# Lora feed-forward with its first sum two tiles ahead, and an earlier key projection in attention

## The chip, the core and the metric

The kernel runs on one core of one Trainium2 chip. Its engines are TensorE (PE), VectorE (DVE), ScalarE (ACT) and GpSimd (POOL); SyncE (SP) only issues transfers here. Each works through its own instructions in order, and they wait for one another on semaphores. The metric is the device time of one execution in microseconds (us).

## What is computed

Two decoder layers over 2048 tokens of width 256, each an attention and a feed-forward, every one with a layer norm ahead and a residual sum behind. The change touches the feed-forward of the first layer (experts that are low-rank additions to one shared weight, two experts a token) and the start of the second layer's attention (16 heads of 128).

```python
# first layer, feed-forward
probs = jax.nn.softmax(x @ Wr + br, axis=-1)
w, idx = jax.lax.top_k(probs, K)                     # K = 2 experts of 8
base_h1 = x @ W1 + b1                                # 256 -> 1024
t1 = jnp.einsum('td,erd->ter', x, A1)                # rank 16
l1 = jnp.einsum('ter,efr->tef', t1, B1) * SCALING
a = gelu_new(base_h1[:, None, :] + l1)
ca = a * combine[:, :, None]
mix = ca.sum(axis=1)
t2 = jnp.einsum('tef,erf->ter', ca, A2)
l2 = jnp.einsum('ter,edr->td', t2, B2) * SCALING
out = mix @ W2 + combine.sum(-1, keepdims=True) * b2 + l2
...
# second layer, attention
q = _mxfp4_matmul(x, wq_codes, wq_scales) + bq       # codes * scales of 32 rows
k = _mxfp4_matmul(x, wk_codes, wk_scales) + bk
v = _mxfp4_matmul(x, wv_codes, wv_scales) + bv
scores = jnp.einsum('bqhd,bkhd->bhqk', q, k) / jnp.sqrt(jnp.float32(HEAD_DIM))
attn = jax.nn.softmax(scores, axis=-1)
out = jnp.einsum('bhqk,bkhd->bqhd', attn, v).reshape(B, S, NUM_HEADS * HEAD_DIM)
return _mxfp4_matmul(out, wo_codes, wo_scales) + bo
```

## The kernel before

The program is a row of stages: the first layer's attention, the Lora feed-forward (`lora_ffn`, its main part runs from about 294 to 521 us), the second attention (`attention`, from 521 us nearly to the end), the last feed-forward. A stage begins when all engines have ended the one before. Products whose precision matters are three matmuls of halves (`three`, L930 to L932: high by high, high by low, low by high).

**The main part of `lora_ffn`** works on four blocks `b` of 512 tokens, and in each on eight tiles `f` of 128 hidden features. Every tile needs two gelus, one for each of the token's two experts. Both are taken from one bank of PSUM, and the second is reached by adding to the first. TensorE does it with `first(f)` (nine matmuls: shared weight plus the first expert's low-rank part), and, when ScalarE has taken the first gelu, `second(f)` (three matmuls that add the second expert minus the first). Then ScalarE takes the second gelu. VectorE multiplies both by the gates (L1400) and adds them into `mix` (L1405), always both gelus of tile f and then `mix` of f. TensorE's `down_rank(f)` (L1322, two matmuls) needs both weighed gelus of tile f; it stands two tiles behind. When all eight tiles are through, TensorE multiplies `mix` by the second weight (L1346) and closes each of four row groups with a product of `t2` (L1350), and begins the next block.

The order is written out by hand. On TensorE it is

```python
first(0)
for f in range(NF):
    if f + 1 < NF:
        first(f + 1)
    second(f)
    if f >= 2:
        down_rank(f - 2)
```

On ScalarE it is both gelus of tile 0, both of tile 1 and so on, with three guests in blocks 1 to 3: after tile 1 a square root (`norm.deviation`, L93), which needs another table of functions, so that a table is loaded ahead of it and the gelu's again behind it; after tile 3 four normalised rows (L109); after tile 5 two copies (L124).

**Beside it, in the same 227 us, weights of the next attention are prepared** in 32 pieces, four (q, k, v, o) for each pair of heads. SP loads a piece (L1243, four L1246) into one of two buffers, GpSimd scales and splits it (`make_whole` L1270, `split_piece` L1278 and L1280; every other piece also two instructions of a bias, L1286, L1289), SP stores it (L1251) and loads the next but one. Of each o piece VectorE adds a product to `v_bias` (`weigh_bias`, L1390), and SP may not overwrite the buffer before: it waits for `v_bias_steps` with all later loads behind the wait. On VectorE `weigh_bias` stands ahead of tile 1 and ahead of tile 5 of each block (from block 0's tile 5 on), and its first instruction waits until GpSimd has scaled that piece.

**The start of `attention`.** TensorE projects the queries and keys of the first block of tokens (`project(0, 0, 0)`, `project(1, 0, 0)`), ScalarE and VectorE take the high and the low halves (`at_q_hi`, `at_q_lo`; the keys' halves bear the name `sw_gate_up_hi` and `_lo`, since they share that memory), and then step 0 begins: scores of queries 0 by keys of block 0, then the keys of block 1 (`project(1, 0, 1)`), then one product of `v_bias` (L1749). Step 1 begins with a wait for VectorE's sum `at_bo` and eight transposes (L117). A projection writes to one of two banks in turn, and waits until VectorE has read what was there two jobs ago (`claim`).

## Time and profile before

| | us |
|---|---|
| median of three runs | 2754.81 |
| lowest and highest | 2754.06, 2755.05 |
| the profiled execution | 2757.06 |
| its span, first to last instruction | 2755.3 |
| TensorE busy in the span | 2629.4 |
| four blocks of `lora_ffn`'s main part | 53.8, 57.6, 57.3, 58.0 |
| from there to the first score of step 1 of attention | 19.0 |

The span lies 1.8 us under the time of its execution, and that execution 2.25 us above the median. The views used are: busy time by stage, the waits summed by who waited for whom, and the order in time of each engine. In the last, a row is one or several equal instructions (`x4`; a matmul of whole float32 numbers counts twice), its start, its length from the first start to the last end, and in brackets the idle time ahead of it and what ended that. Ends of matmuls are modelled and overlap the next start; the distance of two starts is what one costs.

### The profile page before, as it was taken

Reading aid. Unit: us, or ns where it says so; the run is one execution under the profiler, and the core shown is the slowest. Engines: PE = TensorE matmul, PEld = TensorE weight load, DVE = VectorE, ACT = ScalarE, POOL = GpSimd, SP = SyncE. Lnnn points to the kernel's source line nnn. Section 1 sums busy time; section 2 is a strip of 40 time slices with the busy share of each in tenths; the row PEclk is TensorE's granted clock in tenths of the full one; section 3 lists DMA queues with packets and bytes.
Section 4 is the critical chain, followed back from the end, with each engine's and each line's share of the span. In section 5 each row is a group of like instructions: output and inputs, shape, how many; then the busy total and the mean of one; then the engine's idle time right before and its main releaser. Section 6 shows DMA issues by size and latency. Waiting matters only on the chain. (4 is left out here: it accounts for less than half of the span.)

```text
span 2755.3 us, 32467 instructions
## 1 busy us (share of the span) xinstructions
PE 2629.4 (95%) x11020; PEld 1871.1 (68%) x11021; DVE 2042.3 (74%) x2932; ACT 1618.5 (59%) x1891; POOL 2098.4 (76%) x1075
## 2 busy tenths in 40 slices
PE   7886999899999999999999999999999999997998
PEld 3333676677777777777777777777777777764765
DVE  6766655578888888888888888888888888885211
ACT  2323223367767776776677677767767766774122
POOL 2533555559988998998899899889988998996433
PEclk9998899999999999999999999999999999999999
DMA  2001445300000000000000000000000000004621
GB/s 68 0 0 54 122 131 145 114 16 5 8 5 19 6 8 16 5 9 5 16 5 12 16 5 9 5 16 5 12 12 9 8 5 9 1 20 83 228 61 47
DMA packets 76126, 90.52 MB, mean 33 GB/s; under 512 B 9310, under 2 KB 64865, under 8 KB 75970
## 3 DMA queue, kind: packets, MB, share of 16 engines
q1 hardware_dynamic: 72994, 81.30, 10.3%
q0 software_dynamic: 2976, 7.22, 0.9%
q8 instruction: 87, 1.43, 0.2%
q14 instruction: 69, 0.57, 0.1%
HBM read 62.39 MB, written 27.02 MB: 32 GB/s over the span
## 5 line engine op out<-in xcount | busy, mean ns | idle before, releaser
L1876 DVE TENSOR_TENSOR at_top<-at_psum_s,at_top 128x512 f32<-128x512 f32 x960 | 662.7, 690 | 214.9 <-ACT at_prob L1783 193.6
L1783 ACT ACTIVATE at_prob<-at_psum_s 128x1024 f32<-128x1024 f32 x512 | 521.5, 1019 | 451.8 <-PE at_psum_s L932 448.7
L2004 POOL TENSOR_TENSOR at_p_lo<-at_prob,at_p_hi 128x1024 fp32r<-128x1024 f32 x256 | 615.8, 2405 | 0.6 <-ACT at_p_hi L1797 0.6
L1865 DVE TENSOR_TENSOR at_prob<-at_prob,at_psum_m 128x1024 f32<-128x1024 f32 x512 | 603.6, 1210 | 0.0
L1789 ACT ACTIVATE at_prob<-at_prob 128x1024 f32<-128x1024 f32 x512 | 537.7, 1050 | 16.1 <-DVE at_prob L1865 13.0
L2033 POOL TENSOR_TENSOR at_acc<-at_acc,at_prob 128x1024 f32<-128x1024 f32 x189 | 452.9, 2396 | 82.3 <-ACT at_prob L1789 72.5
L1701 PE MATMUL at_psum_o<-at_prob,at_v 128*128 128x512 f32 x1024 | 482.0, 593 | 1.8 <-DVE at_oT_lo L1897 1.4
L2037 POOL TENSOR_TENSOR at_acc<-at_acc,at_prob 128x1024 f32<-128x1024 f32 x189 | 454.1, 2403 | 0.0
L930 PE MATMUL at_psum_s<-at_q_hi,sw_gate_up_hi 128*128 128x512 f32 x1024 | 403.4, 394 | 3.4 <-DVE sw_gate_up_lo L1857 3.4
L932 PE MATMUL at_psum_s<-at_q_hi,sw_gate_up_lo 128*128 128x512 f32 x1024 | 401.7, 392 | 0.0
L931 PE MATMUL at_psum_s<-at_q_lo,sw_gate_up_hi 128*128 128x512 f32 x1024 | 401.3, 392 | 0.0
L930 PE MATMUL at_psum_o<-at_p_hi,at_v_hi 128*128 128x512 f32 x512 | 298.3, 583 | 7.2 <-POOL at_p_lo L2004 6.9
L1701 PEld LDWEIGHTS at_psum_o<-at_prob,at_v 128*128 128x128 f32 x1024 | 184.9, 189 | 138.3 <-issue 118.4
L1797 ACT ACTIVATE at_p_hi<-at_prob 128x1024 fp32r<-128x1024 f32 x256 | 271.1, 1059 | 8.3 <-PE at_psum_o L932 0.2
L2028 POOL TENSOR_TENSOR at_acc<-at_prob 128x1024 f32<-128x1024 f32 x63 | 151.6, 2406 | 123.5 <-ACT at_prob L1789 119.3
L932 PEld LDWEIGHTS at_psum_s<-at_q_hi,sw_gate_up_lo 128*128 128x128 f32 x1024 | 192.9, 188 | 44.0
L930 PEld LDWEIGHTS at_psum_s<-at_q_hi,sw_gate_up_hi 128*128 128x128 f32 x1024 | 193.1, 189 | 40.8 <-DVE sw_gate_up_lo L1857 4.3
L931 PEld LDWEIGHTS at_psum_s<-at_q_lo,sw_gate_up_hi 128*128 128x128 f32 x1024 | 193.0, 188 | 36.4
L932 PE MATMUL at_psum_o<-at_p_hi,at_v_lo 128*128 128x512 f32 x512 | 202.0, 395 | 0.0
L931 PE MATMUL at_psum_o<-at_p_lo,at_v_hi 128*128 128x512 f32 x512 | 200.2, 391 | 0.0
L930 PEld LDWEIGHTS at_psum_o<-at_p_hi,at_v_hi 128*128 128x128 f32 x512 | 96.5, 189 | 89.0 <-issue 50.5
L1909 DVE SCALAR_TENSOR_TENSOR x_tok<-at_psum_w,at_rsum,x_tok 128x256 f32<-128x256 f32 x256 | 111.6, 478 | 52.8 <-PE at_psum_w L932 52.8
(349 smaller groups left out, 4415.8 us busy)
## 6 DMA issues: line engine op xcount, KB each, us to landing
ef_gate_up<-in_ef_gate_up SPq DMA_DIRECT2D x8, 1024.0 KB, 15.2
at_wq_split<-lf_pieces SPq DMA_DIRECT2D x8, 512.0 KB, 3.1
at_wk_split<-lf_pieces SPq DMA_DIRECT2D x8, 512.0 KB, 3.5
at_wv_split<-lf_pieces SPq DMA_DIRECT2D x8, 512.0 KB, 2.9
at_wo_split<-lf_pieces SPq DMA_DIRECT2D x8, 512.0 KB, 4.7
ef_down<-in_ef_down SPq DMA_DIRECT2D x8, 512.0 KB, 13.9
ef_rows_in<-ef_zeros SPq DMA_DIRECT2D x23, 128.5 KB, 8.6
ef_rows<-ef_rows_in SPq DMA_DIRECT2D x23, 128.5 KB, 2.2
```

The source lines that it names most:

```text
L930: nc.tensor.matmul(out, a_hi, b_hi, start=start, stop=False, **kw)
L931: nc.tensor.matmul(out, a_hi, b_lo, start=False, stop=False, **kw)
L932: return nc.tensor.matmul(out, a_lo, b_hi, start=False, stop=stop, **kw)
L1701: nc.tensor.matmul(psum_o[:], v[:, plain_at[kt], half], prob[u % 2][:, kt, :], start=(c == 0 and t == PAIRED[c]), stop=False)
L1783: nc.scalar.activation(pair(u, c, half), psum_s[:, 2 * half:2 * half + 2, :], ACT.Copy).then_inc(kept, 1)
L1789: nc.scalar.activation(part, part, ACT.Exp, scale=SCALE).then_inc(exp_done, 1)
L1797: nc.scalar.activation(p_hi[:, at:at + PAIRED[c], :], prob[u % 2][:, c * KPC:c * KPC + PAIRED[c], :], ACT.Copy).then_inc(p_hi_ready, 1)
L1865: nc.vector.tensor_tensor(part, part, psum_m[:].unsqueeze(1).to_broadcast([P, 2, BT]), ALU.subtract).then_inc(shifted, 1)
L1876: nc.vector.tensor_tensor(top[:, u % 2, :], psum_s[:, t, :], top[:, u % 2, :], ALU.max).then_inc(maxed, 1)
L2004: nc.gpsimd.tensor_tensor(p_lo[:, at, :], part, p_hi[:, at, :].bitcast(F32), ALU.subtract).then_inc(p_lo_ready, 1)
L2033: nc.gpsimd.tensor_tensor(acc2[:], acc2[:], pair(u, c, 0), ALU.add).then_inc(summed, 1)
L2037: nc.gpsimd.tensor_tensor(acc2[:], acc2[:], pair(u, c, 1), ALU.add).then_inc(summed, 1)
```

## The change

In `lora_ffn`, TensorE does `first(0)`, `first(1)`, and then for each f `first(f + 2)`, `second(f)`, `down_rank(f - 2)`. ScalarE takes its gelus in the order in which TensorE gives them: first of 0, first of 1, second of 0, first of 2, second of 1, and so on. The counts for which each engine waits follow from three small functions. The guests on ScalarE stand behind the same f of the loop as before. VectorE's and GpSimd's order stays. In `attention`, `project(1, 0, 1)` is moved from behind the scores of step 0 to ahead of them; ScalarE and VectorE take its result in the same place as before.

```diff
+            def first_at(f):
+                return f if f < 2 else 2 * f - 2
+
+            def second_at(f):
+                return 2 * f + 3 if f < NF - 2 else NF + f
+
+            def gelu_at(f, j):
+                return (f if f < 2 else 2 * f - 1) if j == 0 else min(2 * f + 2, 2 * NF - 1)
...
                         def first(f):
                             if b * NF + f >= 4:
-                                pe.wait_ge(h_ready, 2 * (b * NF + f - 4) + 2)
+                                before, at = divmod(b * NF + f - 4, NF)
+                                pe.wait_ge(h_ready, before * 2 * NF + gelu_at(at, 1) + 1)
...
-                            pe.wait_ge(h_ready, b * 2 * NF + 2 * f + 1)
+                            pe.wait_ge(h_ready, b * 2 * NF + gelu_at(f, 0) + 1)
...
                         first(0)
+                        first(1)
                         for f in range(NF):
-                            if f + 1 < NF:
-                                first(f + 1)
+                            if f + 2 < NF:
+                                first(f + 2)
                             second(f)
                             if f >= 2:
                                 down_rank(f - 2)
...
-                    def gelu(b, n, f, j):
-                        act.wait_ge(h_psum, b * 2 * NF + n + 1)
+                    def gelu(b, f, j):
+                        act.wait_ge(h_psum, b * 2 * NF + (first_at, second_at)[j](f) + 1)
                         if b * NF + f >= RING:
                             act.wait_ge(ranked, b * NF + f - RING + 1)
                             act.wait_ge(mixed, b * NF + f - RING + 1)
...
                     for b in range(NB):
+                        gelu(b, 0, 0)
+                        gelu(b, 1, 0)
                         for f in range(NF):
-                            gelu(b, 0 if f == 0 else 2 * f - 1, f, 0)
-                            gelu(b, 2 * f + 2 if f + 1 < NF else 2 * NF - 1, f, 1)
+                            gelu(b, f, 1)
+                            if f + 2 < NF:
+                                gelu(b, f + 2, 0)
...
-                                dve.wait_ge(h_ready, b * 2 * NF + 2 * f + j + 1)
+                                dve.wait_ge(h_ready, b * 2 * NF + gelu_at(f, j) + 1)
...
                     project(0, 0, 0)
                     project(1, 0, 0)
+                    project(1, 0, 1)
...
-                        if s < 3:
+                        if 1 <= s < 3:
                             project(1, 0, s + 1)
```

TensorE at the end of a block of `lora_ffn`, before: the last three matmuls of `first(7)` and all of `second(6)` stand ahead of `down_rank(4)` (L1322).

```order
L930 MATMUL lf_psum_h<-lf_low_hi,lf_B1T_hi 128x512
L931 MATMUL lf_psum_h<-lf_low_lo,lf_B1T_hi 128x512
L932 MATMUL lf_psum_h<-lf_low_hi,lf_B1T_lo 128x512
L930 MATMUL lf_psum_h<-lf_low_hi,lf_B1T_hi 128x512
L931 MATMUL lf_psum_h<-lf_low_lo,lf_B1T_hi 128x512
L932 MATMUL lf_psum_h<-lf_low_hi,lf_B1T_lo 128x512
L1322 MATMUL lf_psum_t2<-lf_hidden,lf_A2T 128x512 x2
L930 MATMUL lf_psum_h<-lf_low_hi,lf_B1T_hi 128x512
L931 MATMUL lf_psum_h<-lf_low_lo,lf_B1T_hi 128x512
L932 MATMUL lf_psum_h<-lf_low_hi,lf_B1T_lo 128x512
L1322 MATMUL lf_psum_t2<-lf_hidden,lf_A2T 128x512 x6
```

The same place now, from `down_rank(3)` (L1333) on: `second(6)` and `down_rank(4)`, `second(7)` and the last three `down_rank`.

```order
L1333 MATMUL lf_psum_t2<-lf_hidden,lf_A2T 128x512 x2
L930 MATMUL lf_psum_h<-lf_low_hi,lf_B1T_hi 128x512
L931 MATMUL lf_psum_h<-lf_low_lo,lf_B1T_hi 128x512
L932 MATMUL lf_psum_h<-lf_low_hi,lf_B1T_lo 128x512
L1333 MATMUL lf_psum_t2<-lf_hidden,lf_A2T 128x512 x2
L930 MATMUL lf_psum_h<-lf_low_hi,lf_B1T_hi 128x512
L931 MATMUL lf_psum_h<-lf_low_lo,lf_B1T_hi 128x512
L932 MATMUL lf_psum_h<-lf_low_hi,lf_B1T_lo 128x512
L1333 MATMUL lf_psum_t2<-lf_hidden,lf_A2T 128x512 x6
```

`first(7)` has left this stretch: it stands ahead of `second(5)` now, and the block's start has `first(1)` and `first(2)` ahead of `second(0)`, where before only `first(1)` was. The work of a block is the same.

ScalarE from the start of block 0 to the square root of block 1 (L93), before:

```order
L1360 ACT_TABLE_LOAD
L1360 ACTIVATE lf_hidden<-lf_psum_h,lf_b1 128x512 [waits lf_h_psum] x8
L1360 ACTIVATE lf_hidden<-lf_psum_h,lf_b1 128x512 [waits lf_mixed,lf_ranked,lf_h_psum] x12
L93 ACT_TABLE_LOAD
L93 ACTIVATE bn_rstd<-bn_mean_var,bn_eps 128x4 [waits ln_moments_ready]
L1360 ACT_TABLE_LOAD [waits lf_mixed,lf_ranked]
```

And now:

```order
L1372 ACT_TABLE_LOAD
L1372 ACTIVATE lf_hidden<-lf_psum_h,lf_b1 128x512 [waits lf_h_psum] x7
L1372 ACTIVATE lf_hidden<-lf_psum_h,lf_b1 128x512 [waits lf_mixed,lf_ranked,lf_h_psum]
L1372 ACTIVATE lf_hidden<-lf_psum_h,lf_b1 128x512 [waits lf_h_psum]
L1372 ACTIVATE lf_hidden<-lf_psum_h,lf_b1 128x512 [waits lf_mixed,lf_ranked,lf_h_psum] x13
L93 ACT_TABLE_LOAD
L93 ACTIVATE bn_rstd<-bn_mean_var,bn_eps 128x4 [waits ln_moments_ready]
L1372 ACT_TABLE_LOAD [waits lf_mixed,lf_ranked]
```

The square root stood behind 20 gelus (16 of block 0, the four of tiles 0 and 1 of block 1); it stands behind 22 now, the first gelus of tiles 2 and 3 are ahead of it as well.

TensorE at the end of step 0 of attention, before: behind the last score matmul (L932 into `at_psum_s`) the keys of block 1.

```order
L932 MATMUL at_psum_s<-at_q_hi,sw_gate_up_lo 128x512
L930 MATMUL at_psum_w<-x_hi,at_w_hi 128x512
L931 MATMUL at_psum_w<-x_lo,at_w_hi 128x512
L932 MATMUL at_psum_w<-x_hi,at_w_lo 128x512
L930 MATMUL at_psum_w<-x_hi,at_w_hi 128x512
L931 MATMUL at_psum_w<-x_lo,at_w_hi 128x512
L932 MATMUL at_psum_w<-x_hi,at_w_lo 128x512
L1749 MATMUL at_psum_o<-v_bias,at_ones 128x256
```

And now:

```order
L931 MATMUL at_psum_s<-at_q_lo,sw_gate_up_hi 128x512
L932 MATMUL at_psum_s<-at_q_hi,sw_gate_up_lo 128x512
L1765 MATMUL at_psum_o<-v_bias,at_ones 128x256
L117 MATMUL at_psum_o<-ident,at_prob1 128x128
L117 MATMUL at_psum_m<-ident,at_prob1 128x128
```

The six matmuls stand ahead of the first score now, where 18 matmuls into `at_psum_w` follow one another in place of 12.

## Rows read from the trace of the kernel before

**Rows 1.** The page: the span, and TensorE's busy time.

```profile
span 2755.3 us, 32467 instructions
PE 2629.4 (95%) x11020; PEld 1871.1 (68%) x11021; DVE 2042.3 (74%) x2932; ACT 1618.5 (59%) x1891; POOL 2098.4 (76%) x1075
```

**Rows 2.** Busy time by stretch: blocks 1 and 3; PEclk is the granted clock.

```profile
348.12:405.71 57.59, 54.68 (x211) 39.24 (x209) 32.94 (x47) 16.15 (x25) 36.30 (x33) 0.97 0.51 146
...
462.97:520.97 58.00, 55.06 (x210) 39.13 (x208) 34.83 (x49) 16.15 (x25) 34.04 (x30) 0.97 0.45 136
```

**Rows 3.** TensorE's waits, 290 to 520 us: total, times, longest.

```profile
PE lf_psum_h L930 <- ACT lf_hidden L1360: 6.9, 3, 2.3
```

**Rows 4.** Waits of SP's queue, 290 to 530 us: total, times, longest.

```profile
SPq L1243 <- DVE v_bias L1390: 46.4, 4, 15.9
```

**Rows 5.** TensorE in order of time, block 1.

```profile
350.39 0.40 PE L930 MATMUL lf_psum_h<-x_hi,lf_w_hi 128*128 128x512 f32 x1
...
352.49 0.39 PE L930 MATMUL lf_psum_h<-lf_low_hi,lf_B1T_hi 128*128 128x512 f32 x1
...
360.54 0.67 PE L930 MATMUL lf_psum_h<-lf_low_hi,lf_B1T_hi 128*128 128x512 f32 x1 [2.29 <-ACT lf_hidden L1360]
...
367.50 1.88 PE L1322 MATMUL lf_psum_t<-lf_hidden,lf_A2T 128*128 128x512 f32 x4
...
372.00 1.88 PE L1322 MATMUL lf_psum_t<-lf_hidden,lf_A2T 128*128 128x512 f32 x4
...
384.32 3.60 PE L1322 MATMUL lf_psum_t<-lf_hidden,lf_A2T 128*128 128x512 f32 x8
388.53 1.98 PE L1322 MATMUL lf_psum_t<-lf_hidden,lf_A2T 128*128 128x512 f32 x4 [0.62 <-DVE lf_hidden L1400]
```

**Rows 6.** Busy time by stretch, behind that wait; the granted clock stands third last.

```profile
362.00:364.00 2.00, 2.00 (x4) 0.87 (x3) 1.15 (x2) 1.27 (x2) 0.00 (x0) 0.50 0.73 136
```

**Rows 7.** ScalarE in order of time, block 1.

```profile
356.90 1.28 ACT L93 ACT_TABLE_LOAD   x1
...
359.80 0.69 ACT L1360 ACTIVATE lf_hidden<-lf_psum_h,lf_b 128x512 f32<-128x512 f32 x1
```

**Rows 8.** VectorE in order of time, block 1.

```profile
357.19 0.98 DVE L1390 SCALAR_TENSOR_TENSOR v_bias<-lf_whole,lf_v_cols,v_bias 128x256 f32<-128x256 f32 x2
...
376.00 2.25 DVE L1390 SCALAR_TENSOR_TENSOR v_bias<-lf_whole,lf_v_cols,v_bias 128x256 f32<-128x256 f32 x2
...
382.83 1.15 DVE L1400 TENSOR_TENSOR lf_hidden<-lf_hidden,lf_weights 128x512 f32<-128x512 f32 x1 [1.29 <-ACT lf_hidden L1360]
...
386.79 1.69 DVE L1400 TENSOR_TENSOR lf_hidden<-lf_hidden,lf_weights 128x512 f32<-128x512 f32 x2
```

**Rows 9.** SP's queue in order of time: the first load of block 1.

```profile
358.19 0.39 SPq L1243 DMA_DIRECT2D lf_whole<-in_at_wk_codes  x1
```

**Rows 10.** GpSimd in order of time, block 1: the o piece scaled.

```profile
373.80 1.73 POOL L1270 TENSOR_TENSOR lf_whole<-lf_whole,lf_scales 128x512 f32<-128x512 f32 x1
```

**Rows 11.** VectorE in order of time, block 0: both gelus of tile 7.

```profile
328.42 2.35 DVE L1400 TENSOR_TENSOR lf_hidden<-lf_hidden,lf_weights 128x512 f32<-128x512 f32 x2
```

**Rows 12.** TensorE in order of time, start of attention.

```profile
528.73 0.40 PE L932 MATMUL at_psum_w<-x_hi,at_w_lo 128*128 128x512 f32 x1
530.96 0.48 PE L930 MATMUL at_psum_s<-at_q_hi,sw_gate_up_hi 128*128 128x512 f32 x1 [1.84 <-DVE sw_gate_up_lo L1857]
...
532.46 0.63 PE L931 MATMUL at_psum_s<-at_q_lo,sw_gate_up_hi 128*128 128x512 f32 x1
...
535.39 0.40 PE L930 MATMUL at_psum_w<-x_hi,at_w_hi 128*128 128x512 f32 x1
...
539.11 0.33 PE L117 MATMUL at_psum_o<-ident,at_prob 128*128 128x128 f32 x1 [1.73 <-DVE at_bo L1952]
...
540.27 0.39 PE L931 MATMUL at_psum_s<-at_q_lo,sw_gate_up_hi 128*128 128x512 f32 x1
```

**Rows 13.** VectorE in order of time, start of attention: the low half of the queries.

```profile
529.41 0.75 DVE L1857 SCALAR_TENSOR_TENSOR at_q_lo<-at_psum_w,at_cols,at_q_hi 128x512 fp32r<-128x512 f32 x1 [5.13 <-ACT at_q_hi L1774]
```

## Prediction

> **What bounds the kernel now.** I read the page first: TensorE is busy for 2629.4 of 2755.3 us [rows 1], so a microsecond that TensorE loses or gains in a stage moves the end, unless something else holds that stage. Then the busy time by stretch: the changed part of the Lora feed-forward takes 57.6 to 58.0 us for each of blocks 1 to 3 [rows 2], and block 0 has no square root on ScalarE. Then TensorE's waits in that part: it waited for a gelu three times, 2.3 us each, 6.9 in all [rows 3]. In order of time this is one place a block: `second(2)` starts at 360.54 after 2.29 us without work [rows 5], because ScalarE was away from 356.90 to 359.80 with two table loads and a square root, and took the gelu of tile 2 only then [rows 7]. Behind it the granted clock was 0.50, the lower of TensorE's two levels (1.2 GHz, the other is 2.4) [rows 6]. So the wait costs twice. From its end to the pair at 367.50 TensorE took 6.96 us; the same work at full clock is `second` (0.70 us, a third of the 2.10 between the start of `first` at 350.39 and that of the next `second` at 352.49) and one round of the loop (367.50 to 372.00, 4.50), together 5.20. The clock took 1.76, wait and clock 4.05 a block, 12.2 in three [rows 5].
>
> But this is not what the block's end hangs on alone. The last pair of matmuls of `down_rank` starts at 388.53, and the two pairs ahead started at 384.32. A pair costs 1.70 (the round of 4.50 less 2.10 and 0.70), so TensorE was ready at 387.72 and stood some 0.8 us for VectorE, 0.62 by the row, whose ends are modelled [rows 5]. VectorE ended the multiplies of tile 7 at 386.79 + 1.69 = 388.48 [rows 8]. So VectorE holds the block's tail already, and a gain of 4.05 on TensorE alone would only lengthen that wait.
>
> **What holds VectorE.** Go back along its rows. From 376.00 (`weigh_bias` ahead of tile 5) to 388.48 it takes 12.48 us, with one gap of 1.29 for a gelu [rows 8]. And 376.00 is where GpSimd allows it: the o piece was scaled at 373.80 + 1.73 = 375.53, a slack of 0.47 [rows 10]. GpSimd's pieces hang on SP's loads, and these stood 15.9 us behind SP's wait for VectorE's `weigh_bias` ahead of tile 1 [rows 4]: that one ended at 357.19 + 0.98 = 358.17, and SP issued the next load at 358.19 [rows 8, 9]. So there is a chain through four engines: block start, `weigh_bias` ahead of tile 1, SP, transfers, GpSimd (three pieces), `weigh_bias` ahead of tile 5, tiles 5 to 7 on VectorE, last `down_rank`, the products with `mix`, next block.
>
> **The change part by part, block 1 with its start at 348.12 [rows 2].**
> Removed: the wait of 2.29 and its clock, since `second(2)` now needs a gelu that ScalarE took ahead of the square root. On TensorE alone that is -4.05.
> Moved: ahead of `second(0)` stands one `first` more, 2.10 us [rows 5]. VectorE needs the second gelu of tile 0 for everything behind it, so `mix`, the four statistics and `weigh_bias` ahead of tile 1 come 2.10 later: they start 9.07 + 2.10 = 11.17 after the block's start and end at 12.15. SP, with its loads queued behind that wait, goes on 2.10 later too.
> From the end of `weigh_bias` to the scaled o piece it was 375.53 - 358.17 = 17.36. Nothing in it waits for TensorE, so I keep it: 12.15 + 17.36 = 29.51.
> `weigh_bias` ahead of tile 5 can start at 29.56. VectorE gets there earlier (TensorE is further by then), so it now stands and waits there, with tiles 5, 6 and 7 behind, and TensorE's last three `down_rank` behind those.
> From there to the last multiply of tile 7: 12.48 as before at most; 11.19 at least, since the gap of 1.29 was a wait for a gelu that is ready now. So the release of the last `down_rank` lies at 40.75 to 42.04; before it was 388.48 - 348.12 = 40.36. That is +0.4 to +1.7 a block. I take +0.7, near the lower end because the gap's cause is gone, not at it because VectorE's work slides beside GpSimd's there and both are long when they meet (`weigh_bias` took 0.98 while GpSimd stood still, 2.25 beside it [rows 8]).
> TensorE is ready for the last `down_rank` at 387.72 - 348.12 - 4.05 = 35.6, and released at about 41.1. These 5.5 us of standing fall on the last three pairs: the pair of tile 6 can't start before VectorE is through with it (382.83 + 1.15 is 7.98 behind 376.00, less the gap 6.69, so 36.3), the last not before 41.1; so one wait of 3 us stands among them. A wait of 2.3 [rows 3, 5] and one of 1.84 at the start of attention were followed by the lower clock, one of 1.73 just behind that was not: the score matmul at 540.27 is 0.39 long, the one at 532.46 was 0.63 [rows 12]. So I take one fall of the clock a block at the price seen, +1.76, now on the products with `mix`, which are on the path. It could be nothing (if the waits come in pieces, or the slow time falls into them) or two falls, 3.5.
> A block then is 0.7 + 1.76 = +2.5 longer, three blocks +7.4. The 4.05 saved higher up are swallowed by the same wait and give nothing.
> Block 0 has no square root and no long wait of SP. There, tile 7 was weighed at 328.42 + 2.35 = 330.77 [rows 11]; `second(5)` comes 2.10 later, `second(6)` and `second(7)` not, and VectorE has both gelus of 6 and 7 when it had them. I take +0.2, between 0 and +1.
> The rest of ScalarE's new order costs nothing: a first gelu of tile f + 2 must now wait for `down_rank(f - 2)`, 1.70 us behind `second(f)`, but TensorE needs it a whole round (4.50) later.
>
> The clock, weighed once more. The rows say that a wait of 2.3 was followed by half the clock each time. The Trainium skill, "TensorE: Matmul & The Clock Gate", section "HAM oscillation — how this bites in real kernels", says that a loop which waits once a pass falls back each pass and pays for the rise each time. By that rule the fall comes in all three blocks, 5.3 of the 7.6 in my sum; by the row of the 1.73 wait alone it would be nothing, and the sum 2.3.
>
> **Attention.** Before, TensorE ended the keys of block 0 at about 528.96, stood 1.84 until 530.96, and did 12 score matmuls until 535.39: 4.43 us where full speed is 12 x 0.234 = 2.8 (the row at 532.46 has 0.63 against 0.40 at full clock) [rows 12]. Now six matmuls (1.40) go ahead. They need the bank of the queries, which VectorE has read at 529.41 + 0.75 = 530.16 [rows 13], so they fill 530.2 to 531.6, and the scores start 0.64 later. Step 1 starts with VectorE's `at_bo`, which follows the end of the scores, and the six matmuls taken away there stood ahead of a wait of 1.73 anyway, so their going gives nothing [rows 12]. If the clock falls as before, the scores end 0.7 later and so does step 1: +0.7. If the shorter idle time spares the fall, they end at 534.4, 1.0 earlier: -0.9. Neither has a better row than the other; I take 0.
>
> **The sum:** 0.2 + 3 x 2.46 + 0 = +7.6. Against the profiled execution that is 2757.06 + 7.6 = 2764.7, against the median of the runs, 2.25 lower, 2762.4.
>
> **The rivals.**
> Faster, -12.2, 2742.6: the piece chain doesn't hold the block, say because SP's restart is no later or VectorE catches up beside GpSimd, and TensorE's 4.05 a block come through. For it: TensorE's wait and the slow clock are real and surely go. Against it: the slack of 0.47 at 376.00 and the wait at 388.53 [rows 5, 8, 10]. It would need both `weigh_bias` of a block some 4 us earlier. Chance 0.11.
> Within the measurement, +2.3, 2757.1 (0.4 to 1.7 a block makes +1.4 to +6): the chain holds, but TensorE's waits come in pieces and the clock stays up or is down only while it waits. Chance 0.30.
> Slower than forecast, 0.2 + 3 x (1.7 + 3.5) = +15.8, 2770.6: the waits on two of the last `down_rank` bring two falls a block. Chance 0.07.
> That the change doesn't do what it says is no case of its own: the order on TensorE is what the change tells, only a gelu held up by `down_rank` could bring the old wait back, and that has 2.8 us of room.
>
> **How the numbers follow.** Forecast 0.52, the three rivals 0.11, 0.30 and 0.07. Between no change and the measurement's grain, about 0.2% or 5.5 us, lies the second rival; forecast and third are above: slower 0.59, same 0.30, faster 0.11. The lower bound is the chain at +0.4 a block with no fall and attention at -0.9, with 2 us of error in it, 2753; the upper 1 + 3 x (1.7 + 1.76) + 0.7 = +12.1 with one more fall, 2768. Outside lie the faster rival and part of the slowest, under 0.2.
>
> **What would show it.** In the trace after: no wait of TensorE at `second(2)`; SP's longest waits for `v_bias` 2 us longer than 15.9 from a given block's end; VectorE idle 2 to 4 us ahead of `weigh_bias` of tile 5 with GpSimd as releaser; TensorE idle about 5.5 us in all ahead of the last three `down_rank`, with VectorE as releaser; granted clock 0.50 in the products with `mix`; blocks of 59 to 61 us where there were 57.6. The forecast is wrong if VectorE doesn't wait at tile 5, which would mean that the 17.36 isn't fixed, or if blocks 1 to 3 come out at 54 us.

## The result

The changed kernel takes 2767.39 us (median of six executions, 2763.28 to 2769.24) against 2755.14 for the kernel before, run beside it (six, 2754.06 to 2756.83): a ratio of 1.0035, 95% interval 1.0025 to 1.0046. It is slower, by 7 to 13 us; the two medians by themselves lie 12.3 us apart (1.0044), near the upper end of that interval. The forecast was 2762.4, that is +7.6, in a range of 2753 to 2768. Other executions of both kernels later gave 1.0032 (1.0021 to 1.0044).

The profiled execution of the changed kernel took 2763.28 us and is the fastest of its six, so its trace shows less loss than the median: +6.2 us of span, of which 1.6 arose ahead of the changed part (its first matmul into `lf_psum_h` starts at 295.90, before at 294.32). The page, the counterpart of [rows 1]:

```profile
span 2761.5 us, 32467 instructions
PE 2628.7 (95%) x11020; PEld 1870.3 (68%) x11021; DVE 2035.3 (74%) x2932; ACT 1619.6 (59%) x1891; POOL 2094.1 (76%) x1075
```

TensorE is busy 0.7 us less than before in a span that is 6.2 us longer: it waits more, it does not work more. The waits, 290 to 540 us (who waited for whom: total, times, longest), the counterpart of [rows 3, 4]:

```profile
PE lf_psum_t L1333 <- DVE lf_hidden L1415: 13.5, 8, 2.8
...
DVE v_bias L1405 <- POOL lf_whole L1280: 21.5, 4, 6.5
```

```profile
SPq L1253 <- DVE v_bias L1405: 51.2, 4, 18.9
```

The wait for the gelu of tile 2 (6.9 us) is gone. In its place TensorE waits 13.5 us in all for VectorE ahead of `down_rank` (1.4 before). SP's longest wait grew from 15.9 to 18.9.

Blocks 1 to 3 by stretch, with the granted clock third last, the counterpart of [rows 2]:

```profile
350.50:409.07 58.57, 53.36 (x211) 38.38 (x209) 30.33 (x47) 16.38 (x25) 31.91 (x30) 1.00 0.53 135
409.07:465.57 56.50, 53.33 (x210) 38.37 (x209) 29.98 (x47) 16.38 (x25) 35.85 (x32) 1.00 0.53 150
465.57:525.65 60.08, 54.96 (x210) 39.07 (x208) 33.83 (x49) 16.39 (x25) 34.27 (x30) 0.97 0.47 140
```

Block 1 in order of time, the chain that the prediction followed: VectorE's two `weigh_bias` and the multiplies of tile 7, then SP's load, GpSimd's o piece, and TensorE's last `down_rank` pairs (counterparts of [rows 5, 8, 9, 10]; start, length, idle time ahead and what ended it).

```profile
361.69 0.97 DVE L1405 SCALAR_TENSOR_TENSOR v_bias<-lf_whole,lf_v_cols,v_bias 128x256 f32<-128x256 f32 x2
380.99 2.34 DVE L1405 SCALAR_TENSOR_TENSOR v_bias<-lf_whole,lf_v_cols,v_bias 128x256 f32<-128x256 f32 x2 [5.89 <-POOL lf_whole L1280]
...
390.00 1.84 DVE L1415 TENSOR_TENSOR lf_hidden<-lf_hidden,lf_weights 128x512 f32<-128x512 f32 x2
```

```profile
362.69 0.39 SPq L1253 DMA_DIRECT2D lf_whole<-in_at_wk_codes  x1
```

```profile
379.68 1.28 POOL L1280 TENSOR_TENSOR lf_whole<-lf_whole,lf_scales 128x512 f32<-128x512 f32 x1 [0.57 <-DMA lf_scales<-in_at_wo_scales]
```

```profile
384.79 1.99 PE L1333 MATMUL lf_psum_t<-lf_hidden,lf_A2T 128*128 128x512 f32 x4 [2.08 <-DVE lf_hidden L1415]
387.26 1.98 PE L1333 MATMUL lf_psum_t<-lf_hidden,lf_A2T 128*128 128x512 f32 x4 [0.48 <-DVE lf_hidden L1415]
391.89 1.98 PE L1333 MATMUL lf_psum_t<-lf_hidden,lf_A2T 128*128 128x512 f32 x4 [2.65 <-DVE lf_hidden L1415]
```

`weigh_bias` ahead of tile 1 starts 11.19 us after the block's start (350.50); 11.17 was worked out. VectorE then stands 5.9 us for the o piece at tile 5, and TensorE 5.2 us in three pieces for VectorE.

The start of attention, the counterpart of [rows 12]:

```profile
535.57 0.50 PE L930 MATMUL at_psum_w<-x_hi,at_w_hi 128*128 128x512 f32 x1 [2.03 <-DVE at_q_lo L1873]
...
537.08 0.39 PE L930 MATMUL at_psum_s<-at_q_hi,sw_gate_up_hi 128*128 128x512 f32 x1
...
543.69 0.33 PE L117 MATMUL at_psum_o<-ident,at_prob 128*128 128x128 f32 x1 [3.29 <-DVE at_bo L1968]
...
545.21 0.63 PE L931 MATMUL at_psum_s<-at_q_lo,sw_gate_up_hi 128*128 128x512 f32 x1
```

The scores of step 0 run at full clock now (0.39 long), so the stretch from the last product of `lora_ffn` to step 1 is 0.3 us shorter (18.04 against 18.30). But TensorE then waits 3.29 for `at_bo` where it waited 1.73, and the scores of step 1 are 0.63 long, which costs 1.5 us (from their start to the keys behind them 4.35 us, before 2.83).

### The profile page after: what moved, and what is told of

Same layout as the page of the kernel before. It is cut to its first block and busy times, and to the rows that moved or that the text cites. A ratio compares the mean times of both kernels' runs of the same rounds, so it can differ in the third digit from the quotient of the medians.

```text
span 2761.5 us, 32467 instructions
## 1 busy us (share of the span) xinstructions
PE 2628.7 (95%) x11020; PEld 1870.3 (68%) x11021; DVE 2035.3 (74%) x2932; ACT 1619.6 (59%) x1891; POOL 2094.1 (76%) x1075
## 5 line engine op out<-in xcount | busy, mean ns | idle before, releaser
L932 PE MATMUL at_psum_s<-at_q_hi,sw_gate_up_lo 128*128 128x512 f32 x1024 | 401.5, 392 | 0.0
L932 PEld LDWEIGHTS at_psum_s<-at_q_hi,sw_gate_up_lo 128*128 128x128 f32 x1024 | 192.9, 188 | 44.0
L932 PE MATMUL at_psum_o<-at_p_hi,at_v_lo 128*128 128x512 f32 x512 | 202.0, 395 | 0.0
```

What stands on the lines that cost most here:

```text
L932: return nc.tensor.matmul(out, a_lo, b_hi, start=False, stop=stop, **kw)
```

## The theories

A, the forecast's: a chain of pieces (`v_bias` on VectorE, SP's loads, three pieces on GpSimd, `v_bias` again) sets the end of each Lora block; the change made its start 2.1 us later, and the low clock behind TensorE's longer waits adds to that. B: VectorE's own work in the block's tail, slowed by GpSimd beside it, sets the end, and the chain has room. C: only the falls of the clock cost. D: the attention part costs. Each ratio in the table compares a kernel with runs of the kernel before on the same chip, with its 95% interval. The last column has the three blocks in the one trace of each kernel, with a star where the granted clock fell to 0.50, and two where it fell twice or stayed down for longer. Block 3 is counted to its last product (57.84 for before, where [rows 2] has 58.00).

| kernel | ratio to before (interval) | blocks 1 to 3 in its trace, us |
|---|---|---|
| before | 1 | 57.59* 57.26* 57.84* |
| changed | 1.0035 (1.0025 to 1.0046) | 58.57 56.50 60.08* |
| Lora part alone | 1.0021 (1.0011 to 1.0032) | 60.35* 56.51 61.10* |
| attention part alone | 1.0000 (0.9991 to 1.0010) | 57.65* 57.60* 57.11 |
| changed, early `weigh_bias` | 0.9962 (0.9947 to 0.9976) | 53.74 53.09 54.01 |
| before, early `weigh_bias` | 0.9990 (0.9980 to 1.0000) | 55.10 55.07 55.30 |
| the same again | 0.9979 (0.9970 to 0.9989) | 56.77* 55.07 55.87 |
| changed, `second(0)` back | 1.0017 (1.0004 to 1.0029) | 60.33** 55.42 57.10 |
| Lora part, early `weigh_bias` | 0.9964 (0.9951 to 0.9978) | 53.16 56.44* 55.28 |
| changed, late `weigh_bias` | 1.0027 (1.0013 to 1.0040) | 61.82** 57.27* 61.32* |
| `second(0)` back, early `weigh_bias` | 0.9971 (0.9962 to 0.9981) | 52.93 53.99 54.26 |
| changed, again | 1.0032 (1.0021 to 1.0044) | 61.20** 61.33** 61.75** |
| changed, bias rows moved on GpSimd | 1.0027 (1.0017 to 1.0036) | 58.84* 58.64* 59.56 |
| before, again (one execution) | | 58.27* 57.72* 57.84* |

## Which part costs

The changed kernel with its attention part undone:

```diff
                     project(0, 0, 0)
                     project(1, 0, 0)
-                    project(1, 0, 1)
...
-                        if 1 <= s < 3:
+                        if s < 3:
                             project(1, 0, s + 1)
```

> The changed order of the Lora feed-forward alone; attention as in the kernel before. If the whole cost comes from the Lora blocks (blocks 1 to 3 of 58.6, 56.5 and 60.1 us against 57.6, 57.3 and 57.8, and block 0 of 54.6 against 53.8), this is 7 to 11 us slower than before, within 2 us of the changed kernel. If the attention part is what costs (its step 1 waited 3.29 us for VectorE's at_bo where it waited 1.73, and the clock fell behind that), it is only 3 to 7 us slower than before, and the changed kernel is 3 us or more above it. If clock falls behind TensorE's long waits decide, the trace shows 1 to 3 stretches at granted clock 0.5 in the tails of blocks 1 to 3.

Measured: 1.0021, some 5.8 us (3 to 9). And the other part alone, the kernel before with this diff reversed:

> The attention part alone; Lora feed-forward as before, so blocks of 53.8, 57.6, 57.3 and 57.8 us. My forecast had 0 for this part, between -0.9 and +0.7. If the clock falls behind the longer wait for at_bo as in the trace of the changed kernel, +1 to +1.5; if the scores run at full clock and nothing falls later, -0.9. By the rival that the attention part carries the loss, +4 or more.

Measured: 1.0000, within 2.8 us either way. Its trace has the same two effects as the changed kernel's: 0.9 us gained up to step 1, then the low clock.

```profile
539.41 0.33 PE L117 MATMUL at_psum_o<-ident,at_prob 128*128 128x128 f32 x1 [3.29 <-DVE at_bo L1953]
...
540.70 0.63 PE L931 MATMUL at_psum_s<-at_q_lo,sw_gate_up_hi 128*128 128x512 f32 x1
```

So D falls: the attention part is worth nothing that can be measured. The loss is in the Lora part. The two ratios together make 1.0021, while the whole was 1.0035; so the changed kernel itself was run again:

> The changed kernel itself once more, beside a run of before with fresh executions. The first comparison gave a ratio of 1.0035 (six executions each); its Lora part alone gave 1.0021 and its attention part alone 1.000. If the two parts add, this comes out at 1.002 to 1.003, below the first figure but inside both intervals; if they don't add (attention costs only behind the changed Lora part), it stays at 1.0035 or above.

Measured: 1.0032. That is above the sum of the parts, but the intervals overlap (the Lora part alone reaches to 1.0032). Whether 3 us more come from the two together stays open.

## Does the chain of pieces hold the block?

The move frees the chain early: VectorE does `weigh_bias` ahead of tile 0, where it stands waiting for a gelu anyway (for 2.40 us in block 1 of the changed kernel).

```diff
-                            if (b * NF + f) % 4 == 1 and b * NF + f >= 5:
+                            if (b * NF + f) % 8 in (0, 5) and b * NF + f >= 5:
                                 weigh_bias((b * NF + f) // 4 - 1)
```

> The changed kernel, with VectorE's weigh_bias in blocks 1 to 3 moved from ahead of tile 1 to ahead of tile 0, so that SP's next loads, and GpSimd behind them, start about 10 us earlier in a block. If the chain of pieces (v_bias, SP, transfers, GpSimd, v_bias) holds the block, VectorE waits no more at tile 5, TensorE's tail waits of 5 us go, and blocks 1 to 3 come out at 54 to 55.5 us: 7 to 13 us faster than before, 17 to 24 faster than the changed kernel. If it was VectorE's and GpSimd's own work in the tail that holds the block (they slow each other where they work side by side), blocks stay at 57 us or more and the time is within 5 us of before. If only the clock falls cost, the gain is at most 5 us on the changed kernel.

Measured: 0.9962, 10.5 us faster than before (7 to 15). The blocks by stretch, and VectorE at tile 5 of block 1:

```profile
349.04:402.78 53.74, 52.81 (x211) 38.55 (x209) 35.37 (x47) 16.37 (x25) 39.33 (x33) 1.00 0.61 157
402.78:455.87 53.09, 52.82 (x211) 38.54 (x209) 33.67 (x47) 16.37 (x25) 34.44 (x30) 1.00 0.54 156
```

```profile
374.84 1.35 DVE L1405 SCALAR_TENSOR_TENSOR v_bias<-lf_whole,lf_v_cols,v_bias 128x256 f32<-128x256 f32 x2
```

No wait stands ahead of `weigh_bias` at tile 5, and TensorE is busy for 52.82 of 53.09 us in block 2: it is the bound. VectorE and GpSimd do the same instructions as in the changed kernel, and yet the block is shorter by more than 3 us, so B falls as the theory of the whole. (How long the two take side by side does matter behind the chain; the section on the clock has it.) C falls too: block 2 is 3.4 us shorter than the changed kernel's block 2, and neither has a fall of the clock. The same diff on the kernel before is the control:

> The same move of weigh_bias, on the kernel before: a control. There TensorE's wait for the gelu of tile 2 (2.3 us) and the low clock behind it (1.8) stay, so freeing the chain of pieces can only take away the last wait for VectorE (0.6 to 0.8 a block): 0 to 2.5 us faster, blocks of 57 us. If it is as fast as the changed order with the same move, then the early weigh_bias by itself makes the gain and the changed order gives nothing.

Measured: 0.9990, 2.8 us faster (0 to 5.5); its repeat further down gave 0.9979, 5.8 us (3 to 8), which is more than was expected. Under the same freed chain the changed order is 0.28% faster than the old one by the first of these, 7.7 us, and 0.17% by the repeat, 4.7 us. So the changed order does save time on TensorE, but only once the chain is out of the way; without that its gain is swallowed and the delay of the chain's start shows. Of the 10.5 us, 3 to 6 are the move's own.

The blocks of the control missed the expectation: 55.1 to 55.3 us where 57 was expected, because the clock didn't fall in them, and because the chain had held the old blocks too. The trace of the attention part alone has a block 3 of the old order without a fall. It took 57.11 us, only 0.5 less than its two blocks with one, and VectorE stood there for the o piece:

```profile
492.33 2.34 DVE L1390 SCALAR_TENSOR_TENSOR v_bias<-lf_whole,lf_v_cols,v_bias 128x256 f32<-128x256 f32 x2 [2.43 <-POOL lf_whole L1270]
```

With attention as before, the changed order with the early `weigh_bias` (the diff of the first experiment and this move together):

> The changed order of the Lora feed-forward with weigh_bias ahead of tile 0 in blocks 1 to 3, and attention as in the kernel before. The run with the changed attention gave a ratio of 0.9962 to before, blocks of 53.1 to 54.0 us and no clock fall in them. With attention as before the blocks must be the same; if the moved key projection costs or gives nothing in time, the ratio is 0.995 to 0.997; if it costs 1.5 us as one trace showed (a longer wait for at_bo and a fall behind it), 0.9945 to 0.996.

Measured: 0.9964, equal to 0.9962; the attention part is worth nothing here either. The trace has a clock fall in block 2 that the other lacked.

## How much of the 2.1 us passes through the chain?

One `first` ahead of `second(0)` made the chain's start later. Put back:

```diff
                         for f in range(NF):
+                            if f == 0:
+                                second(f)
                             if f + 2 < NF:
                                 first(f + 2)
-                            second(f)
+                            if f:
+                                second(f)
```

(with `first_at(2)` 3 and `second_at(0)` 2).

> The changed kernel, with second(0) put back ahead of first(2) on TensorE; ScalarE's gelus follow in the same order as in the changed kernel. So the one first of 2.10 us no longer stands ahead of the second gelu of tile 0, and VectorE's weigh_bias ahead of tile 1 starts near 9.1 us after a block's start, not 11.2; TensorE's wait at second(2) should stay away. If the 2.1 us on the chain of pieces are what made the change slow, VectorE waits about 2 us less at tile 5 and blocks 1 to 3 are 1 to 2.5 us shorter than in the changed kernel: 56 to 58 us, and the time lies within 3 us of before. If the chain isn't the cause, it stays where the changed kernel is, 6 to 10 us above before.

Measured: 1.0017, about half of the changed kernel's loss, though the intervals overlap (this one is 1.0004 to 1.0029). It is 4.7 us above before, where "within 3 us" was expected. And the opposite, `weigh_bias` one tile later:

```diff
-                            if (b * NF + f) % 4 == 1 and b * NF + f >= 5:
+                            if (b * NF + f) % 8 in (2, 5) and b * NF + f >= 5:
```

> The changed kernel, with weigh_bias in blocks 1 to 3 one tile later, ahead of tile 2: the opposite of the early move. VectorE then does it behind the multiplies and the sum of tile 1, 2 to 3 us later. If the chain of pieces sets the block's end, each of blocks 1 to 3 is 2 to 3 us longer than in the changed kernel, 60 to 63 us, and the time is 5 to 9 us above the changed kernel's, a ratio to before of 1.004 to 1.007. If the chain has slack or VectorE's own work is the bound, nothing changes against the changed kernel.

Measured: 1.0027, no slower than the changed kernel. That is a miss of the expectation, and the traces show a reason. GpSimd in block 2, from the k piece scaled to the o piece scaled: first with `second(0)` back (block start 408.03), then the changed kernel (409.07), then with the late `weigh_bias` (408.05).

```profile
423.86 1.82 POOL L1280 TENSOR_TENSOR lf_whole<-lf_whole,lf_scales 128x512 f32<-128x512 f32 x1 [17.03 <-DMA lf_scales<-in_at_wk_scales]
...
435.17 1.26 POOL L1280 TENSOR_TENSOR lf_whole<-lf_whole,lf_scales 128x512 f32<-128x512 f32 x1
```

```profile
427.50 1.61 POOL L1280 TENSOR_TENSOR lf_whole<-lf_whole,lf_scales 128x512 f32<-128x512 f32 x1 [14.31 <-DMA lf_scales<-in_at_wk_scales]
...
437.29 1.27 POOL L1280 TENSOR_TENSOR lf_whole<-lf_whole,lf_scales 128x512 f32<-128x512 f32 x1
```

```profile
428.32 1.29 POOL L1280 TENSOR_TENSOR lf_whole<-lf_whole,lf_scales 128x512 f32<-128x512 f32 x1 [20.16 <-DMA lf_scales<-in_at_wk_scales]
...
437.03 1.28 POOL L1280 TENSOR_TENSOR lf_whole<-lf_whole,lf_scales 128x512 f32<-128x512 f32 x1
```

| block 2, us from its start | `second(0)` back | changed | late `weigh_bias` |
|---|---|---|---|
| first `weigh_bias` ends | 10.05 | 12.15 | 14.07 |
| k piece starts on GpSimd | 15.83 | 18.43 | 20.27 |
| k piece to o piece scaled | 12.57 | 11.06 | 9.99 |
| o piece scaled | 28.40 | 29.49 | 30.26 |
| second `weigh_bias` starts | 28.44 | 29.53 | 30.30 |
| from there to the block's end | 26.98 | 26.97 | 26.97 |
| block | 55.42 | 56.50 | 57.27 |

The last three rows are theory A: in these three blocks the end comes 26.97 us after the second `weigh_bias` can start, whatever stood ahead. (They are three of the five blocks in which VectorE's part of that took its shortest time; in others it was up to 31.8, which the section on the clock takes apart.) But the chain is elastic. GpSimd does the same nine instructions in 12.6, 11.1 or 10.0 us, because VectorE comes to a stand ahead of tile 5 and then leaves it alone (k scaled in 1.82 beside VectorE, in 1.29 alone). Of 2.1 us at the chain's start 1.1 arrive at its end, of the next 1.9 only 0.8. Blocks 1 and 3 of the same traces scatter about that (1.9 and 2.3 arrive in the first execution of the changed kernel, 1.0 and 1.4 in the second); in the first GpSimd stood 0.57 and 1.15 us there for the o piece's scales, in block 2 not at all. The two remedies together:

> second(0) back ahead of first(2), and weigh_bias ahead of tile 0 in blocks 1 to 3; attention as changed. If nothing but TensorE holds the block once the pieces are early, the place of second(0) makes no difference: blocks of 53 to 54 us and a ratio of 0.995 to 0.997, as with the early weigh_bias on the changed order. If VectorE's later start on tile 0 still matters, it is up to 2 us faster than that, 0.994 to 0.996.

Measured: 0.9971 (0.9962 to 0.9981), no better than the early `weigh_bias` alone. With the chain out of the way the place of `second(0)` is worth nothing that can be measured. The last attempt on the chain shortened GpSimd's part of it:

```diff
                     for p in range(len(PIECES)):
-                        if p % 2 == 0:
+                        if p % 4 == 0:
                             add_bias(p // 2)
+                            add_bias(p // 2 + 1)
```

> The changed kernel, with GpSimd's two bias instructions that stood between the k and the v piece moved ahead of the q piece (L1296 and L1299; both pairs of a group of four pieces stand together there). In block 2 of the changed kernel these two held GpSimd from 22.73 to 24.93 us after the block's start, 2.2 us between the loads that SP issued and the scaled o piece. If the chain through GpSimd holds the block, VectorE's wait ahead of weigh_bias of tile 5 falls from 5.3 to 3 to 3.8 us, blocks 1 to 3 are 1.5 to 2.2 us shorter, and the time is 4 to 7 us below the changed kernel's: 0.9995 to 1.001 of before. If VectorE's work behind it is the bound instead, nothing moves.

Measured: 1.0027, which can't be told from the changed kernel's 1.0032; 0.9995 to 1.001 was expected if the chain through GpSimd holds the block, so that was missed. GpSimd's v piece came 2.2 us earlier, but then GpSimd stood for the o piece's scales:

```profile
435.87 1.27 POOL L1280 TENSOR_TENSOR lf_whole<-lf_whole,lf_scales 128x512 f32<-128x512 f32 x1 [1.24 <-DMA lf_scales<-in_at_wo_scales]
```

The second `weigh_bias` of block 2 started 29.24 us after the block's start instead of 29.53, so this edit moved the chain by 0.3 us only. It neither supports nor contradicts A; it shows that behind GpSimd the transfers are the next link.

## The clock

In the forecast one fall of the clock a block, 1.76 us, was the larger term. The traces of the changed kernel and of its second run have the same block 2 up to 444.6 us (both blocks start within 0.02 us of one another), and then part. First execution, TensorE, VectorE and GpSimd:

```profile
448.40 1.98 PE L1333 MATMUL lf_psum_t<-lf_hidden,lf_A2T 128*128 128x512 f32 x4 [1.55 <-DVE lf_hidden L1415]
450.22 3.62 PE L1358 MATMUL lf_psum_d<-lf_w,lf_mix 128*128 128x256 f32 x16
```

```profile
444.84 0.69 DVE L1420 TENSOR_TENSOR lf_mix<-lf_hidden 128x512 f32<-128x512 f32 x1
...
446.65 1.70 DVE L1415 TENSOR_TENSOR lf_hidden<-lf_hidden,lf_weights 128x512 f32<-128x512 f32 x2
```

```profile
445.10 1.57 POOL L1280 TENSOR_TENSOR lf_whole<-lf_whole,lf_scales 128x512 f32<-128x512 f32 x1 [2.04 <-DMA lf_scales<-in_at_wq_scales]
```

Second execution:

```profile
450.57 3.78 PE L1333 MATMUL lf_psum_t<-lf_hidden,lf_A2T 128*128 128x512 f32 x4 [3.74 <-DVE lf_hidden L1415]
454.14 4.50 PE L1358 MATMUL lf_psum_d<-lf_w,lf_mix 128*128 128x256 f32 x16
458.48 0.59 PE L1362 MATMUL lf_psum_d<-lf_B2T,lf_t 128*128 128x256 f32 x2
```

```profile
444.82 1.66 DVE L1420 TENSOR_TENSOR lf_mix<-lf_hidden 128x512 f32<-128x512 f32 x1
...
447.61 2.91 DVE L1415 TENSOR_TENSOR lf_hidden<-lf_hidden,lf_weights 128x512 f32<-128x512 f32 x2
```

```profile
444.67 1.26 POOL L1280 TENSOR_TENSOR lf_whole<-lf_whole,lf_scales 128x512 f32<-128x512 f32 x1 [1.64 <-DMA lf_scales<-in_at_wq_scales]
```

```profile
453.00:455.00 2.00, 2.00 (x5) 1.01 (x4) 0.61 (x2) 0.00 (x0) 1.50 (x3) 0.50 0.81 273
```

A transfer landed 0.43 us earlier, so GpSimd began the q piece at 444.67, ahead of VectorE's sum (444.82), and not behind it (445.10 against 444.84). The instruction that began first kept its time (GpSimd 1.26; VectorE 0.69), the other was stretched (VectorE 1.66; GpSimd 1.57). VectorE's multiplies of tile 7 then met GpSimd again and ended 2.17 us later. TensorE's wait grew from 1.55 to 3.74, the granted clock fell to 0.50, the lower of the two levels (1.2 GHz, 2.4 above), the pair took 3.57 from start to start instead of 1.82, and the first products 4.34 instead of 3.45. That is 2.17 + 1.75 + 0.89 = 4.8, and the block took 61.33 where it had taken 56.50.

The Trainium skill, "SBUF — State Buffer", section "Who interferes with whom", says that the order of issue, and not the kind of operation, decides which of VectorE and GpSimd is blocked. The trace agrees: 0.69 and 1.57 in one order, 1.66 and 1.26 in the other.

This is the rule and not one case. Five traces have the changed order with its chain unfreed and GpSimd's own order as it was (the changed kernel twice, the Lora part alone, `second(0)` back, late `weigh_bias`). In all their 15 blocks VectorE's sum of tile 6 starts 6.2 us after the second `weigh_bias`. In five of them GpSimd's q piece began behind it; the sum took 0.69, and the last multiply of tile 7 ended 9.7 to 9.8 us after the second `weigh_bias` had started. In ten it began ahead; the sum took 1.64 to 1.66, and the last multiply came after 11.9 us, once after 10.85. Seven of these ten had a wait of 3.7 us ahead of the last `down_rank`, and each of the seven was followed by the lower clock.

A fall of the clock costs nothing where a wait for VectorE stands behind it. That is block 3 of the first execution, TensorE:

```profile
500.09 5.37 PE L1333 MATMUL lf_psum_t<-lf_hidden,lf_A2T 128*128 128x512 f32 x8 [2.33 <-DVE lf_hidden L1415]
508.25 1.98 PE L1333 MATMUL lf_psum_t<-lf_hidden,lf_A2T 128*128 128x512 f32 x4 [2.79 <-DVE lf_hidden L1415]
510.07 3.62 PE L1358 MATMUL lf_psum_d<-lf_w,lf_mix 128*128 128x256 f32 x16
```

```profile
500.00:502.00 2.00, 1.91 (x3) 0.88 (x4) 1.97 (x4) 0.00 (x0) 0.93 (x2) 0.52 0.77 297
510.00:512.00 2.00, 2.00 (x10) 1.71 (x9) 1.69 (x3) 0.00 (x0) 1.92 (x3) 1.00 0.83 83
```

The low clock lay on the pairs of tiles 5 and 6, TensorE stood 2.79 us behind them, and the products ran at full clock. The block's 60.08 come from a later release and from VectorE. So a block is a sum of three parts:

| us, blocks 1, 2, 3 | before | changed | changed, again |
|---|---|---|---|
| block start to second `weigh_bias` | 27.88, 27.89, 27.85 | 30.49, 29.53, 30.72 | 29.54, 29.54, 29.84 |
| from there to the last multiply of tile 7 | 12.48, 12.14, 12.54 | 10.85, 9.75, 11.91 | 11.90, 11.93, 11.91 |
| from there to the block's end | 17.23, 17.23, 17.45 | 17.23, 17.22, 17.45 | 19.76, 19.86, 20.00 |

The chain adds 1.6 to 2.9 us in the first row, VectorE gives 0.2 to 2.4 back in the second, and the clock costs 0 or 2.5 to 2.6 in the third. Blocks of the two traces differ by up to 4.8 us for this reason. How much of the spread of the other executions it makes was not seen in a trace, and the kernel before spreads by 10 us too (2752.7 to 2762.2 in the runs beside the changed kernel's second).

Does a wait of 2.3 always bring the fall, as [rows 3, 6] had it? A second trace of before:

> The kernel before once more, for a second trace. TensorE's waits for the gelu of tile 2 must be there again, 2.3 us in each of blocks 1 to 3. If a wait of 2.3 is always followed by the low clock, all three blocks show a fall and take 57.3 to 57.8 us. In the kernel before with the early weigh_bias the same waits stood in the trace with no fall in any block, so if the fall depends on more than the wait's length, some block of this trace may go without one and be about 1.8 us shorter.

Measured: falls in all three blocks again, 57.7 to 58.3. And a second trace of the kernel before with the early `weigh_bias`:

> The kernel before with the early weigh_bias once more, for a second trace and more executions. Its first trace had TensorE's three waits of 2.3 us but no clock fall in blocks 1 to 3 (55.1, 55.1, 55.3 us), and was the fastest of its 12 executions; their median lay 6.5 us above it. If falls behind these waits come in some executions and not in others, and make up that difference, an execution near the median shows falls in two or three blocks, each 1.8 to 2.5 us longer. If blocks are again 55 us and the execution is near the median, the 6.5 us lie elsewhere in the program.

Measured: 0.9979 (0.9970 to 0.9989), with one fall. TensorE at `second(2)` of blocks 1 and 2, and both blocks by stretch:

```profile
362.16 0.50 PE L930 MATMUL lf_psum_h<-lf_low_hi,lf_B1T_hi 128*128 128x512 f32 x1 [2.29 <-ACT lf_hidden L1360]
...
418.94 0.51 PE L930 MATMUL lf_psum_h<-lf_low_hi,lf_B1T_hi 128*128 128x512 f32 x1 [2.29 <-ACT lf_hidden L1360]
```

```profile
349.74:406.51 56.77, 54.48 (x210) 39.12 (x209) 32.49 (x47) 16.14 (x25) 38.94 (x33) 0.97 0.59 148
406.51:461.58 55.07, 52.77 (x211) 38.47 (x209) 34.61 (x47) 16.16 (x25) 38.86 (x32) 1.00 0.53 153
```

The same wait of 2.29, with a fall in one block and none in the next; the fall costs 56.77 - 55.07 = 1.70. Over the five traces that hold this wait (before twice, the attention part alone, before with the early `weigh_bias` twice) a fall followed 9 times of 15. What decides between them was not isolated. The profiled execution, with its one fall, lies 1.1 us under the median of this run. The 6.5 us between the first trace, without a fall, and its median are more than one fall; that the other executions had two or three was not seen in a trace. So that expectation stays undecided.

## Why the prediction was right

**The wait at `second(2)` goes.** The wait went. What its going is worth on TensorE alone was set too high: 12.2 us for three blocks, with a fall of the clock in each. Under the freed chain the changed order took 160.8 us for the three blocks, the old one 165.5 with no clock fall and 167.7 with one, so 4.6 to 6.9; the ratios give 4.7 to 7.7.

**The chain starts 2.10 us later, at 11.17, and its 17.36 stay.** The start was right (11.19). From the first `weigh_bias` to the o piece scaled it was 18.3 in block 1 (380.96 - 362.66) and 17.3 in block 2; the second `weigh_bias` starts 30.49, 29.53 and 30.72 us after the block's start where 29.56 was worked out. That it agrees so well in block 2 is partly luck: against the order with `second(0)` back only 1.1 of the 2.1 us come through, since GpSimd catches up while VectorE stands. "Nothing in it waits for TensorE, so I keep it" was the weak step. It overlooked that the length of GpSimd's work depends on what VectorE does beside it, and that GpSimd may have to stand for the o piece's scales (0.57 us in block 1, 1.15 in block 3).

**VectorE waits 2 to 4 us at tile 5.** Mis-sized: 5.3 to 6.5 in the profiled execution. It cost nothing, since all of it lies ahead of the same release.

**From there to the last multiply 11.2 to 12.5 us.** The band was too narrow at its lower end: 10.85 in block 1 (391.84 - 380.99), 9.75 in block 2, 11.91 in block 3, and 11.90 to 11.93 in the second execution. The order in which the two engines meet decides.

**TensorE stands 5.5 us ahead of the last three `down_rank`, in pieces.** 5.21 in block 1 (2.08, 0.48, 2.65), 3.17 in block 2, 5.12 in block 3.

**One fall of the clock a block, 1.76.** Wrong as a constant: none, none, and one that cost nothing in the profiled execution; in the second one in all three blocks, on the products with `mix` as forecast, at 2.5 to 2.6 us each. The mean over the six blocks is 1.3. The Trainium skill, "TensorE: Matmul & The Clock Gate", section "HAM oscillation — how this bites in real kernels", has a loop that waits once a pass fall back each pass; that held in 9 of 15 passes for the waits of 2.3 us, and in the changed kernel in 1 of 3 and 3 of 3.

**Block 0: +0.2.** It came out at 54.6 against 53.8, inside the 0 to +1, and at 53.9 in the second execution.

**Attention: 0, with -0.9 and +0.7 as ends.** Right within what can be measured (1.0000, 2.8 us either way). In the trace both ends came: the scores ran at full clock (the -0.9 case), and the longer wait for `at_bo` that took up the rest was followed by a fall of the clock that the forecast did not have, +1.5. That was an omission: the six matmuls taken away ahead of the wait (1.40 us) lengthened it by 1.56, and what a longer wait does to the clock was not asked.

**The size.** +7.6 forecast, +9.6 and +8.8 by the two ratios, +12.3 by the first two medians, +6.2 in the profiled span. The mechanism was right: the chain starts later, the block's end is released later, the saved wait is swallowed. So was the mean of the terms: over the six blocks of both traces the release came 2.1 us later, VectorE's part was 1.0 shorter and the clock cost 1.3, together +2.3 a block, where 1.7, -1.0 and 1.8 made +2.5. As constants they were wrong: single blocks lie between 0.8 us under and 4.1 us over their counterpart. That the profiled span comes near the forecast is luck: its three blocks make only +2.5 of the +7.4 forecast, and 1.6 arose ahead of the changed part. Where the rest of the loss by the ratios lies, beyond some 7 us in the three blocks, stays open.

**The rivals.** The faster one (the chain doesn't hold the block) is excluded: VectorE did stand at tile 5 for the o piece. Of the 12.2 us that it promised, 5 to 8 came when the early `weigh_bias` took the chain really out of the way (changed order against old under the same move). The one within the measurement (waits in pieces, no falls) is what blocks 1 and 2 of the profiled execution did, which is the fastest of its six.

## What to carry to other kernels

Before a wait on the busiest engine is removed, look for the next release behind it that does not depend on it: here a side job (weights of the next stage, through four engines) set the block's end with 0.5 us of slack, and the order that saves 1.5 to 2.6 us a block on TensorE lost time until one instruction pair of that side job was moved to a place where its engine stood idle anyway. Ask of each reordering what else hangs on the result that now comes later; here the second gelu of tile 0 released a whole queue of transfers. The version to keep is the changed order with the early `weigh_bias`, 0.9962 of before.

## What the runs showed that was not expected

The chain of pieces is elastic: the same nine GpSimd instructions took 10.0 to 12.6 us, and of a delay at its start about half arrived in block 2. A transfer 0.43 us earlier made a block 4.8 us longer: 2.2 through the order in which VectorE and GpSimd met, 2.6 through the clock behind the longer wait that followed. A fall of the clock with a wait behind it cost nothing (block 3 of the changed kernel). And a wait of 2.29 us was followed by the lower clock in 9 of 15 cases, not in all.
